# The context of layer 0 from VectorE scans in place of matmuls with a matrix of powers

## What is computed

```python
alpha = exp(-softplus(tau_ctx))
ctx[t] = alpha * ctx[t-1] + x[t]                  # for each batch and channel
wg = sigmoid(concat(x, ctx) @ Wg.T + bg)
gated = x * wg
h1 = gelu(x @ Wn1.T + bn1)
mod = 0.5 + sigmoid(h1 @ Wn2.T + bn2)             # one factor for each of 32 traces
traces[d][t] = decay[d] * traces[d][t-1] + gated[t] * mod[t, d]
temporal = sum over d of softmax(blend)[d] * traces[d]
gate = sigmoid(temporal @ Wtemp.T + btemp)
soma = gelu(x @ Wsoma.T + bsoma)
x = x + layernorm((soma * gate) @ Wout.T) * gamma + beta
x = x + attention(x)                              # layer 1, 16 heads
```

## Time and profile before

| | us |
|---|---|
| runs shown (three) | 373.04, 376.12, 381.86 |
| their median | 376.12 |
| the profiled execution | 372.85 |
| its span, first to last instruction | 371.0 |
| around the span | 1.85 |
| PE busy | 325.0 (88%) |
| DVE busy | 294.9 (79%) |
| POOL busy | 256.6 (69%) |
| ACT busy | 213.4 (58%) |

### The profile page before, as it was taken

How to read it: one execution, slowest core, us unless ns; L and a number is a source line. 1 busy time by engine, 2 the same in 40 slices (tenths; PEclk the granted TensorE clock), 3 DMA queues, 4 the chain that set the end, 5 groups by cost and what they waited for, 6 DMA issues and landing times. The chain is left out here.

```text
span 371.0 us, 10198 instructions
## 1 busy us (share of the span) xinstructions
PE 325.0 (88%) x3287; PEld 227.0 (61%) x3297; DVE 294.9 (79%) x1506; ACT 213.4 (58%) x452; POOL 256.6 (69%) x281
## 2 busy tenths in 40 slices
PE   1749759999999999999987499899699989999994
PEld 0415417657476765757463366778578867887773
DVE  4784998688778777787786876799699979998971
ACT  4742301374735455463735367778578877887872
POOL 2047254296675849486584497699789998999980
PEclk9968976999999999999999789999999999999999
DMA  7200000001000035200254004535643564344011
GB/s 227 57 0 3 28 0 2 29 0 32 0 2 28 3 73 90 37 0 0 46 69 55 3 4 77 95 66 69 119 128 77 77 124 113 94 78 105 3 31 30
DMA packets 23472, 19.23 MB, mean 52 GB/s; under 512 B 2304, under 2 KB 23040, under 8 KB 23424
## 3 DMA queue, kind: packets, MB, share of 16 engines
q1 hardware_dynamic: 23424, 18.63, 25.1%
HBM read 3.94 MB, written 2.10 MB: 16 GB/s over the span
## 5 line engine op out<-in xcount | busy, mean ns | idle before, releaser
L1384 POOL TENSOR_TENSOR arena<-arena,neg_max 128x512 f32<-128x512 f32 x128 | 130.0, 1044 | 20.6 <-DVE neg_max L1258 20.1
L1258 DVE CUSTOM_DVE_ANT_0 arena<-ps,arena 128x128 f32<-128x128 f32 x512 | 113.8, 286 | 16.6 <-PE ps L640 10.8
L919 ACT ACTIVATE arena<-ps 128x512 f32<-128x512 f32 x128 | 69.7, 596 | 17.0 <-PE ps L654 17.0
L1331 POOL TENSOR_TENSOR arena<-decay_a,arena 128x512 f32<-128x512 f32 x32 | 44.5, 1418 | 50.3 <-ACT arena L779 50.3
L654 PE MATMUL ps<-ident_sb,arena 128*128 128x128 f32 x512 | 69.1, 279 | 0.0
L654 PEld LDWEIGHTS ps<-ident_sb,arena 128*128 128x128 f32 x512 | 57.0, 142 | 6.8 <-issue 5.9
L1344 POOL TENSOR_TENSOR arena<-arena 128x448 f32<-128x448 f32 (+6 forms) x56 | 41.9, 749 | 14.7 <-DVE arena L1098 11.8
L1258 DVE DVE_READ_ACCUMULATOR2_ANT neg_max<- 128x1 f32 x512 | 42.5, 83 | 0.0
L670 PE MATMUL ps<-arena 128*32 128x128 f32 x1024 | 42.0, 281 | 0.0
L640 PE MATMUL ps<-arena 48*128 48x128 bf16 x512 | 25.9, 221 | 11.4 <-DVE neg_max L1258 5.7
L1098 DVE TENSOR_TENSOR arena<-ps,arena 128x448 f32<-128x448 f32 (+6 forms) x56 | 23.9, 426 | 14.8 <-PE ps L454 8.7
(11 more groups left out here) (151 smaller groups left out, 591.3 us busy)
## 6 DMA issues: line engine op xcount, KB each, us to landing
arena<-q_parts SPq DMA_DIRECT2D x96, 64.0 KB
arena<-k_parts SPq DMA_DIRECT2D x96, 64.0 KB
arena<-in_x SPq DMA_DIRECT2D x8, 256.0 KB, 2.7
out<-arena SPq DMA_DIRECT2D x8, 256.0 KB, 2.9
arena<-in_consts SPq DMA_DIRECT2D x1, 740.0 KB, 6.4
w_sb<-in_w SPq DMA_DIRECT2D x1, 576.0 KB, 7.4
rows_sb<-in_rows SPq DMA_DIRECT2D x1, 288.5 KB, 2.9
ident_sb<-in_ident SPq DMA_DIRECT2D x1, 64.0 KB, 3.5
```

Of the source, the lines that this page charges most:

```text
L919: act.activation(probT[q % PT_RING], ps[1][:, q % 2, :], ACT.Exp, scale=-1.0)\
L1258: dve.tensor_tensor_reduce(out=neg_t[q % NT_RING][:, cs], in0=ps[0][:, score_bank(c) + slot, cs], in1=nbias[n % 2], scale=1.0, scalar=3.0e ...
L1331: pool.tensor_tensor(mod_a[u][:, b * W:b * W + W].rearrange("p (k d) -> p k d", d=D), decay_a[:], modn[u][:, b * D:b * D + D].unsqueeze(1) ...
L1384: pool.tensor_tensor(t4, t4, neg_max[:, n % 2, 4 * z:4 * z + 4].unsqueeze(2).broadcast_to([P, 4, P]), ALU.subtract).then_inc(s["shifted"], 1)
```

## The change

`alpha` is one exp of one column in the prologue; `lt`, its tables (256 columns of the constants' load) and its two steps are gone. On TensorE `f_context` with its matmuls is gone from `front` and `step`, on ScalarE `f_context` with its copy. VectorE gets an `f_context` that reads `xT` and writes `ctxT` in four scans, one per batch. In a step it stands behind the first `b_states`; in `front` it stands behind the prologue and ahead of `f_gated`. The gate waits for all four scans. VectorE's lines keep their order otherwise. The load of the next x waits for the transposition and for GpSimd's `xb`, no longer for the context.

```diff
-C_LT, C_LTM = 0, P
-C_A = 2 * P
+C_A = 0
...
-        lt = sb("lt", [P, P])
+        alpha = sb("alpha", [P, 1])
...
             def load_x(i, m):
-                sp.wait_ge(s["ctx_ps"], grp(i, m, 1, -1))
+                sp.wait_ge(s["xT_ps"], grp(i, m, 1, -1))
...
-            def f_context(i, m):
-                u = m % 2
-                if at_start(i, m, 1):
-                    pe.wait_ge(s["vec_step"], vec("lt"))
-                four(bank(u, 1), lambda cs: xn[u][:, cs], lambda cs: lt[:], "ctx_ps")
...
             def f_gate(i, m):
...
-                pe.wait_ge(s["ctx_ready"], grp(i, m, 1, 1))
+                pe.wait_ge(s["ctx_ready"], grp(i, m, GB, GB))
...
-            def f_context(i, m):
-                u = m % 2
-                act.wait_ge(s["ctx_ps"], grp(i, m, 1, 1))
-                act.activation(ctxT[u], bank(u, 1), ACT.Copy).then_inc(s["ctx_ready"], 1)
...
-                act.activation(exp_lt, c_sb[:, C_LT:C_LT + P], ACT.Exp, scale=lna[:, D + 1:D + 2])\
-                    .then_inc(s["act_step"], 1)
+                act.activation(alpha[:], lna[:, D + 1:D + 2], ACT.Exp).then_inc(s["act_step"], 1)
...
-            dve.wait_ge(s["act_step"], scal("lt"))
-            pro("lt", dve.tensor_tensor(lt[:], exp_lt, c_sb[:, C_LTM:C_LTM + P], ALU.mult))
...
+            def f_context(i, m):
+
+                u = m % 2
+                if at_start(i, m, 1):
+                    dve.wait_ge(s["act_step"], scal("alpha"))
+                dve.wait_ge(s["xT_ready"], grp(i, m, 1, 1))
+                for b in range(GB):
+                    cs = slice(b * P, b * P + P)
+                    dve.tensor_tensor_scan(ctxT[u][:, cs], alpha[:].broadcast_to([P, P]), xT[u][:, cs], 0.0,
+                                           ALU.mult, ALU.add).then_inc(s["ctx_ready"], 1)
...
             def front(i, m):
+                f_context(i, m)
                 f_gated(i, m)
...
                 b_states(i, m, range(0, 1))
+                f_context(i, m + 1)
                 if closes:
                     c_residual(i, m - 1)
                 b_states(i, m, range(1, 2))
```

More of the change, by code:

```diff
@@ L61 @@
 C_END = C_K + P
-VEC_STEPS = ["neg_abs_tau", "neg_relu_tau", "gate_biases", "mod_bias", "q_bias", "k_bias"] + [f"wn2_row{b}" for b in range(GB)] + ["log_decay", "lt",
+VEC_STEPS = ["neg_abs_tau", "neg_relu_tau", "gate_biases", "mod_bias", "q_bias", "k_bias"] + [f"wn2_row{b}" for b in range(GB)] + ["log_decay",
              "blend_max", "blend_negmax", "decay_arg", "blend_sum", "blend_recip", "blend_4", "half_bw", "decay_p",
@@ L68 @@
              "dense_lam", "cnt_one", "cnt_none"]
-ACT_STEPS = ["exp_tau", "softplus", "lt", "exp_blend", "decay_p", "apow", "decay_a", "exp_u", "w_b3", "w_a1", "w_a3"]
+ACT_STEPS = ["exp_tau", "softplus", "alpha", "exp_blend", "decay_p", "apow", "decay_a", "exp_u", "w_b3", "w_a1", "w_a3"]
 def vec(name):
@@ L208, in build @@
         bl_e, bl_m, bl_s, bl_r, bl_4 = pr[:, 320:352], pr[:, 352:353], pr[:, 353:354], pr[:, 354:355], pr[:, 384:512]
-        exp_lt, exp_p, apow = pr[:, 640:768], pr[:, 768:800], pr[:, 800:808]
+        exp_p, apow = pr[:, 768:800], pr[:, 800:808]
         arg_a = pr[:, 1024:1536]
@@ L224, in build @@
             "small_loaded wn2_loaded const_loaded x_loaded0 x_loaded1 w_loaded idx_loaded vec_step act_step blend_turned "
-            "half_set xT_ps xT_ready ctx_ps ctx_ready wg_ps h1_ps soma_ps gate_tanh h1_ready soma_ready modT_ps "
+            "half_set xT_ps xT_ready ctx_ready wg_ps h1_ps soma_ps gate_tanh h1_ready soma_ready modT_ps "
             "modn_begun modn_ps modT_tanh gated_ready modT_ready modn_ready mod_part1 mod_rest_ready mod_part2 "
@@ L554, in front @@
                 pe.transpose(bank(1, 0)[:, 0:P], bl_4, ident).then_inc(s["blend_turned"], 1)
-                f_context(i, m)
                 f_hidden(i, m)
@@ L564, in step @@
                 f_x(i, m + 1)
-                f_context(i, m + 1)
                 b_states(i, m, range(0, 2))
@@ L994, in _ @@
             pro("log_decay", dve.tensor_tensor(lna, sp_d, sp_c, ALU.subtract))
-            dve.wait_ge(s["act_step"], scal("lt"))
-            pro("lt", dve.tensor_tensor(lt[:], exp_lt, c_sb[:, C_LTM:C_LTM + P], ALU.mult))
             pro("blend_max", dve.tensor_reduce(bl_s, bl, AX_X, ALU.max))
             pro("blend_negmax", dve.tensor_scalar(bl_m, bl_s, -1.0, None, ALU.mult))
+            dve.wait_ge(s["const_loaded"], 16)
             pro("decay_arg", dve.tensor_tensor(arg_a.rearrange("p (k d) -> p k d", d=D),
@@ L1245, in logits @@
                 if q == NT_RING - 2:
-                    dve.wait_ge(s["ctx_ps"], G)
                     dve.wait_ge(s["xT_ps"], G)
@@ L1420, in shape_constants @@
     r = np.arange(P)
-    lag = r[None, :] - r[:, None]
-    c[:, C_LT:C_LT + P] = np.maximum(lag, 0)
-    c[:, C_LTM:C_LTM + P] = lag >= 0
     to_start = np.repeat(np.arange(NCH) * Q, D)[None, :] - r[:, None]
```

## The result

The changed kernel takes 386.67 us, the median of 4 runs (384.71 to 390.35); the kernel before, run beside it, 374.58 (369.14 to 381.86). The ratio is 1.0395, with a 95% interval of 1.0304 to 1.0486: slower. The forecast was 379.7, in a range of 374 to 388. The profiled execution took 384.71 us, its span is 382.9, so 11.9 more than the span of before.

A forecast was written before the change was run, and what follows sets the result against it. TensorE was taken to bound the loop's later steps, VectorE the step of group 1. Front +4.3, group 1 +1.3, group 2 -0.9 and groups 3 to 7 +2.1 gave +6.8 on 372.85: 379.7 us, range 374 to 388.

The forecast's parts named there:

- The scan: On VectorE, each scan takes 0.396 us (residual plus one more pass of 128 columns), four take 1.58 us.
- Groups 3 to 7: At the gate in these steps, TensorE gets the context 0.3 to 0.5 us late: five groups at 0.41, +2.1 us.
- Group 2: In this step VectorE waits for TensorE, so the 0.89 us freed from TensorE is gained whole: -0.9 us.
- Group 1: In this VectorE-bound step, scans 1.58, less 0.7 for an earlier start, plus 0.4 for GpSimd as neighbour: +1.3 us.
- The front: Before the loop, scans stand behind VectorE's prologue and delay gate, modulation and GpSimd's lag sums: +4.3 us.
- The sum for layer 0: Front, group 1, group 2 and groups 3 to 7 together: 4.3 + 1.3 - 0.9 + 2.1 = +6.8 us.
- TensorE's busy time: Sign over all eight groups: TensorE's matmul time down by about 8 x 0.89 us.
- the rivals: Four other outcomes: dearer scans (chance 0.21), streaming scans (0.08), front taken up (0.12), TensorE's gain kept (0.04).
- scans of 0.55 us: Rival at the gate's wait in all groups: scans dearer than two passes, 384.6 us at this size; chance 0.21.
- the front's delay: Rival in the front: idle POOL and TensorE take the delay up, +2.5 in place of +6.8, 375.4 us; chance 0.12.
- The attention should take as long as before: Sign for the attention, behind layer 0: its duration stays unchanged, with no term in the sum.

The follow-up runs named there:

- same_place: Changed kernel with `alpha` in a tile of `lt`'s old size, so other buffers lie where they lay before the change; 383.24 us, ratio 1.0141 to the kernel before.
- three_after: Changed kernel with a third buffer for the attention's stacks; 371.7 us, ratio 0.9867 to the kernel before.
- three_early: three_after with group 0's scans moved ahead, to where VectorE waits for the transposed blend weights; 367.91 us, ratio 0.9829 to the kernel before.
- early_front: same_place with group 0's scans moved ahead in VectorE's prologue, to its wait for the transposed blend weights; 381.52 us, ratio 1.0119 to the kernel before.
- again: The changed kernel run once more, unedited, in another set; 386.54 us, ratio 1.0163 to the kernel before.
- three_hidden: three_early with TensorE and ScalarE doing the hidden layer ahead of the gate; 365.72 us, ratio 0.9758 to the kernel before.
- before_moved: Kernel before with a spare 32-byte tile behind `lt`, moving later buffers' addresses; 370.9 us, ratio 0.9846 to the kernel before.
- before_late: Kernel before, delayed in the front by seven VectorE copies ahead of the first gated product; 381.29 us, ratio 1.0174 to the kernel before.
- code_before: Kernel before with 24, 12 and 28 already-met waits starting TensorE's, ScalarE's and VectorE's programs, moving the attention's code; 375.48 us, ratio 1.0103.

## Why the prediction failed, step by step

**The scan.** Estimated at 0.396 us, bounded by the residual's 0.265 and by 0.92; measured 0.32 (1.28 for four), so below the 0.38 to 0.41 that were to show the forecast right. By the Trainium skill ("DVE: opcode table, instruction layouts, handler registers and perf-mode slots", section on datapath and trigger behaviour) the scan runs at half throughput, which gave the same 0.396. The measured slot is 0.055 above the residual's, where a second pass of 128 columns would be 0.131: by the fixed part used there (0.134) it goes at 0.7 of the residual's rate, not at half. Half rate would fit with a fixed part of 0.06. Scans of one width can't tell the two apart, so no run here shows the rate; the price of 0.396 was too high.

**Groups 3 to 7.** Predicted +0.41 each, by a context that comes 0.3 to 0.5 late. With the shorter scan it came nearly on time: the gate's second matmul starts 4.19 us behind the head in group 4 (114.08 - 109.89), 4.27 to 4.35 in the others, before 4.20 in all five. TensorE idles 0.72 to 0.88 there and not 1.3. Behind that idle time the matmul's two passes take 1.12 us and not 1.02, and the hidden layer starts 1.06 behind it where it started 0.95 behind. Group 7, after; before, L398 started at 172.87 and the hidden layer at 173.82:

```profile
177.69 1.12 PE L390 MATMUL ps<-arena,w_sb 128*128 128x512 f32 x2 [0.82 <-DVE arena L1051]
178.75 0.43 PE L400 MATMUL ps<-arena,cols_sb 128*32 128x128 f32 x8
```

Both together are 0.10 to 0.26 us a group, and the steps are 0.17 longer (84.84 against 84.16 for four). So the loss stands where it was forecast, on TensorE at the gate. From the head of group 3 to the first scores it is 0.8 us in place of 2.1, the term of layer 0 that was most mis-sized.

**Group 2.** Predicted -0.9, no idle time on the scans: it has none, and the head behind it gained 0.67 (4.72 to 4.05).

**Group 1.** Predicted +1.3, measured +0.58 (4.14 to 4.72), by terms that were both off. The price of GpSimd as a neighbour was taken as 0.4 from the earlier trace rows; the profile shows 1.1, four scans in 2.46 beside GpSimd's `xb` (timeline):

```profile
38.79 2.46 DVE L1051 TENSOR_TENSOR_SCAN arena<-alpha,arena 128x128 f32<-128x128 f32 x4
...
38.95 1.38 POOL L1316 TENSOR_TENSOR arena<-arena,rows_sb 128x512 f32<-128x512 f32 x1
```

Beside a free GpSimd they take 1.35. The Trainium skill ("SBUF — State Buffer", section "SBUF: two separate sides") calls the port that these two engines share an exclusive lock, held for a whole instruction. The loss of 1.1, near the 1.38 of GpSimd's one instruction, agrees. The profile shows it on one scan, which took 1.42 us beside the 0.39 of the quickest. What gave the rest back in group 1 wasn't tried. The figures of groups 1 and 2 are those of one execution, and these two steps scatter: between the heads of groups 1 and 3 lie 50.3 to 51.9 us in five profiles with the matmuls (mean 51.1) and 51.7 to 53.2 in nine with the scans (mean 52.3). By the means the two steps lose 1.1 us where +0.4 was forecast; the gain of 0.67 in group 2 isn't there in same_place, three_after and three_early.

**The front.** Predicted +4.3, measured +4.1, and early_front shows its cause: VectorE begins the scans only behind its constants.

**The sum for layer 0** was +6.8; measured 4.9 to the first scores, 4.9 and 5.0 by the two pairs of spans, 5.7 in both pairs of medians. Right in its mechanism, somewhat too high. By the prediction's own price (3.2 us for 0.1 in a scan) the shorter scan alone takes 2.4 off, to +4.4. One more sign missed: TensorE's busy time was to fall by about 7.1 us and fell by 1.8 (325.0 to 323.2), in the pair with three buffers by 3.7 (324.1 to 320.4); where the rest of it went wasn't followed. None of the rivals was it: scans of 0.55 us would have given 384.6, close to the measured time, but the scans are cheaper than forecast, and the front's delay was not taken up.

**The step that failed** is the sentence "The attention should take as long as before". The attention took 7.0 us longer in the profiled execution, in longer waits for stacks (3.0) and behind them in stretches at a lower granted clock (1.5 and 2.2). It hangs on transfers that land 20 to 24 us after their first issue, while TensorE asks for them after 19.4 to 20.0, and the earlier trace rows held no row of it: the waits for stacks, 5.5 us of the span of before, weren't read, since nothing was edited there. Nor was the base safe. The sum stood on one execution of 372.85, while the medians of before in the six sets of runs told of here are 374.6 to 379.1. On those, layer 0's 5.7 gives 380 to 385, and with a third buffer, where no wait is left, the two kernels do differ by 5.7. The rest up to 386.7 is lost at the stack loads; why their waits were longer, and how much of that the change makes, stays open. That 386.67 lies within the stated range is luck: none of the terms of the sum stood for this loss.

## What to carry to other kernels

A part without an edit isn't a constant: where the profile shows waits for transfers that only just land in time, read how far they scatter, price them with the rest, or take them away first and compare then (here one more buffer was worth 2.6% and brought the spread of the changed kernel's runs from 10.5 us, in again, to 3.5). Work moved from a full engine to one with idle time helps where that idle time lies ahead of the consumer; here it lay behind, and what helped was to give the consumer other work first, as three_hidden does (about 0.4 us a step). In a front, ask what the receiving engine is doing at that moment: here four fifths of layer 0's loss was one place in VectorE's order.

## What the runs showed of the hardware

A scan of 128x128 in fp32 on VectorE holds its slot for 0.32 us, 0.055 more than a product with a sum over the same columns. Four of them took 1.1 us longer beside one GpSimd instruction. Twenty-four transfers for a stack, issued one behind the other, landed 19.8 to 24.5 us after the first issue where TensorE waited for it, and the same stack's load landed after 20.1 us in one kernel and 23.6 in the other. Behind waits for stacks of 3.94 and 4.03 us TensorE's granted clock was 0.71 and 0.58 over the next 5.7 and 5.9 us; behind one of 3.14 it was 1.00. The length of the wait alone doesn't decide it: behind waits of 3.29 (early_front) and 3.33 (before_moved) it was 1.00 too, but 0.50 behind one of 3.08 (before_late) and 0.68 behind one of 2.35 (code_before), each over the next 5.2 to 5.6 us. By the marks above these low stretches cost 1.5 and 2.2 us, more than the 3.0 by which the waits themselves had grown.
